# The scan's tile with the place within a chunk outermost

## The reference, cut to what matters

```
Bu = einsum('blh,pht->blpt', x, B_mat)
S = 1 + steps * G
M = [1/S, -alpha/steps, steps/S, 1 - alpha]          # 2x2 per feature
F1 = steps / S * Bu ;  F2 = steps**2 / S * Bu
# state_t = M @ state_{t-1} + (F1_t, F2_t), over the 2048 tokens of a sequence
ys = second component of the state
Cy = einsum('blpt,hpt->blht', ys, C_mat)
out = Cy[..., 0] - Cy[..., 1] + x * D
```

## Time and profile before

| | us |
|---|---|
| median of 3 runs (2365.41 to 2367.84) | 2366.09 |
| the profiled execution, its own time | 2358.44 |
| its span, first to last instruction | 2356.0 |
| PE busy / DVE busy / ACT busy / POOL busy | 2176.4 / 2028.9 / 1542.3 / 671.4 |
| mean granted TensorE clock | 0.956 |

### The profile page before, as it was taken

One profiled execution on the slowest core, in us unless ns is written; L12 is line 12 of the kernel. 1 busy time (PEld: TensorE's weight loads), 2 busy tenths in 40 slices (PEclk: granted clock), 3 DMA queues, 4 the chain that ended last, 5 costly groups with the idle time before them and its releaser, 6 DMA issues. The chain is left out here.

```text
span 2356.0 us, 47793 instructions
## 1 busy us (share of the span) xinstructions
PE 2176.4 (92%) x15828; PEld 1282.4 (54%) x15829; DVE 2028.9 (86%) x5148; ACT 1542.3 (65%) x2993; POOL 671.4 (28%) x997
## 2 busy tenths in 40 slices
PE   4599968999999999999999999999998894999997
PEld 2355544444444444444444544544543783888886
DVE  7799858999999999999999999999991664777775
ACT  3144414678888888888888888888888452444443
POOL 5523002232322322322322322322211254333333
PEclk8799977999999999999999999999999886999999
DMA  5179875654554654432432432433222895444443
GB/s 169 58 217 266 276 179 77 119 118 90 103 107 88 108 107 86 92 84 63 92 85 63 92 78 70 92 76 72 69 89 64 292 307 215 78 81 81 82 81 70
DMA packets 176412, 273.23 MB, mean 116 GB/s; under 512 B 53608, under 2 KB 126072, under 8 KB 170372
## 3 DMA queue, kind: packets, MB, share of 16 engines
q0 software_dynamic: 45840, 137.55, 28.6%
q1 hardware_dynamic: 125332, 122.86, 17.3%
q10 hardware_dynamic: 5044, 10.32, 1.5%
HBM read 128.64 MB, written 140.98 MB: 114 GB/s over the span
## 5 line engine op out<-in xcount | busy, mean ns | idle before, releaser
L1524 ACT ACTIVATE a_p<-banks 128x512 f32<-128x512 f32 x2176 | 1131.2, 608 | 256.8 <-PE banks L1417 206.8
L1577 DVE TENSOR_REDUCE a_mx<-banks 128x1 f32<-128x512 f32 x1536 | 943.4, 680 | 20.1 <-PE banks L1406 20.0
L1485 PE MATMUL banks<-a_p,a_v 128*32 128x512 f32 (+3 forms) x5120 | 589.0, 544 | 1.6 <-ACT a_o L1542 1.1
L1406 PE MATMUL banks<-a_k,a_q 52*128 52x512 f32 (+5 forms) x1600 | 446.8, 413 | 1.9 <-DVE a_rowtop L1574 0.3
L1417 PE MATMUL banks<-a_q,a_k 50*128 50x512 f32 (+7 forms) x1600 | 415.8, 396 | 1.1
L1574 DVE CUSTOM_DVE_ANT_0 a_masked<-banks,a_later 128x512 bf16<-128x512 f32 (+3 forms) x768 | 330.8, 484 | 19.2 <-PE banks L1406 17.3
L1417 PEld LDWEIGHTS banks<-a_q,a_k 54*128 54x128 f32 (+1 forms) x1600 | 227.3, 185 | 198.7 <-DVE a_mx L1577 95.6
L1406 PEld LDWEIGHTS banks<-a_k,a_q 52*128 52x128 f32 (+1 forms) x1600 | 224.1, 185 | 118.0 <-DVE a_mx L1577 55.4
L1406 PE MATMUL banks<-a_k,q 48*128 48x512 f32 (+6 forms) x896 | 256.7, 420 | 6.2 <-DMA a_k<-aug_rows 4.6
L1417 PE MATMUL banks<-q,a_k 50*128 50x512 f32 (+7 forms) x896 | 231.5, 402 | 1.1 <-DVE a_orow L1597 0.3
L1485 PEld LDWEIGHTS banks<-a_p,a_v 128*32 128x32 f32 x5120 | 109.3, 108 | 175.0 <-issue 125.3
(11 more groups left out here) (276 smaller groups left out, 2997.2 us busy)
## 6 DMA issues: line engine op xcount, KB each, us to landing
expert_rows<-a_zeros POOLq DMA_DIRECT2D x132, 258.0 KB, 5.3
a_k<-ka_parts POOLq DMA_DIRECT2D x42, 256.0 KB, 6.3
e_x<-expert_rows SPq DMA_DIRECT2D x71, 129.0 KB, 2.3
expert_rows<-e_y SPq DMA_DIRECT2D x71, 128.0 KB
qa_parts<-m_part SPq DMA_DIRECT2D x16, 512.0 KB
ka_parts<-m_part SPq DMA_DIRECT2D x16, 512.0 KB
va_tiles<-m_va SPq DMA_DIRECT2D x8, 1024.0 KB, 6.8
qb_parts<-m_part SPq DMA_DIRECT2D x16, 512.0 KB, 3.8
```

Source lines behind the costliest of these rows:

```text
L1406: ins = pe.matmul(ps[bank][:, col:col + w], q_op[r % 3][part, p, qt * P:(qt + 1) * P], keys_of(r, k0)[part, kp, k0:k0 + w], start=True, st ...
L1485: ins = pe.matmul(ps_o[VW * h:VW * h + VW, c0:c0 + w], v_op[o][:, kt, hk * VW:hk * VW + VW], prob[:, (at + slot) % NPB, col:col + w], star ...
L1524: nc.scalar.activation(prob[:, (t * NSC + n) % NPB, :], ps[bank][:, :], ACT.Exp, scale=SCALE).then_inc(s_ex, 1)
L1577: ins = v.tensor_reduce(top, ps[bank][:, :], AX.X, ALU.max)
```

## The change

The tile has the same size and place, but its elements are ordered otherwise. Before, token i of chunk c of a partition stood at element 16 c + i. Now it stands at element 256 i + c. A place of all chunks is therefore 256 elements in a row, and the 16 tokens of one chunk are 256 elements (1 KB) apart. Each user of the tile has a view that goes over it in the old order of tokens:

```diff
             def scale(n):
                 act.wait_ge(s_bu, n + 1)
-                nc.scalar.activation(f2[:, n * BT:(n + 1) * BT], bu[n % 2][:, :], ACT.Copy,
+                nc.scalar.activation(by_chunk(f2)[:, n * (BT // CHUNK):(n + 1) * (BT // CHUNK), :],
+                                     bu[n % 2][:, :].rearrange("p (c i) -> p c i", i=CHUNK), ACT.Copy,
                                      scale=C["c2"]).then_inc(s_f, 1)
...
-            f2v = f2[:, :].rearrange("p (c i) -> p c i", i=CHUNK)
+            f2v = by_chunk(f2)
...
+def by_chunk(tile):
+
+    return tile[:, :].rearrange("p (i c) -> p c i", i=CHUNK)
...
-    own = M["f2"][:, :].rearrange("p (b c i) -> p b c i", b=B, i=CHUNK)[:, b, first:first + count, :]
+    own = by_chunk(M["f2"])[:, b * NCH + first:b * NCH + first + count, :]
...
                 for k in range(KD):
-                    pe.matmul(ps[k][:, :], c_mat[:, k * P:(k + 1) * P], y[:, blk * BT:(blk + 1) * BT],
+                    pe.matmul(ps[k][:, :].rearrange("p (c i) -> p c i", i=CHUNK), c_mat[:, k * P:(k + 1) * P],
+                              by_chunk(y)[:, blk * (BT // CHUNK):(blk + 1) * (BT // CHUNK), :],
                               start=True, stop=True).then_inc(s_c, 1)
```

## The result

The changed kernel takes 2374.22 us (median of 7 runs, 2369.08 to 2381.06), the one before 2365.41 (7 runs of its own). The medians are 8.8 us apart. The ratio of the two kernels is given as 1.0042, with a 95% interval from 1.0031 to 1.0053, which is 7.3 to 12.5 us; it is not the quotient of the medians (1.0037). The changed kernel is slower. The forecast was +5.9. Spans are 2368.6 and 2356.0 us.

A forecast was written before the change was run, and what follows sets the result against it. DVE was taken to bound 42 to 72 us, PE the end of `front` and 136.7 to 320 us. Front -7.3, PE's reads +11.8 and POOL's additions +1.4 gave +5.9 us, 2372.0 us; range 2359 to 2380.

The forecast's parts named there:

- The steps on DVE: In `front`: contiguous operands shorten a step from 1.87 to 1.38 us; DVE 7.65 us earlier from L385, range 5.5 to 9.5.
- POOL's part: In `front`: DVE's loss beside POOL's L211, L215 and L217 taken as unchanged, some 2.4 us, from 1 to 5.
- ACT's write: In `front`, before DVE starts: ACT's last write to elements 1 KB apart costs 0.4 us more, once; bounds 0 and 0.43.
- PE's reads: In `middle`: lone words at 1.67 ns cost 0.43 us more a MATMUL, 1.72 a block, +11.8 us in all.
- no cost: Rival for `middle`: PE reads lone words at no cost, hidden by its own pace; -5.9 us, 2360.2; chance 0.23.
- a share of its own cycle: Rival for `middle`: PE pays 0.14 us more a MATMUL, 4.2 us; total -1.7 us, 2364.4; chance 0.1.
- POOL's additions: In `middle`, blocks 0 to 2: L544 and L546 on lone words delay DVE, for which PE waits; +1.4 us, 0 to 5.
- half of 6 x 0.45: In `middle`: six POOL additions in blocks 0 to 2, each 0.45 us longer, half reaching the end: 1.4 us.

The follow-up runs named there:

- TensorE in a row: The changed kernel, with TensorE's first product of a block reading 512 contiguous elements of the normalised input's tile instead of lone words (result wrong): 2359.37 us, ratio 0.9983 to the kernel before.
- the additions in the working tile: The changed kernel, with GpSimd's two additions per block of the carried state going to a contiguous working tile (blocks 1 to 7 lack it): ratio 1.0016 to the kernel before.
- TensorE's lone words alone: The kernel before, with only TensorE's first products reading lone words 1 KB apart, from the normalised input's tile (result wrong): ratio 1.0051, +12.2 us.
- the kernel in fours: The whole computation with four neighbouring tokens side by side, a place of all chunks being every fourth word: 2359.16 us, ratio 1.0005 to the kernel before.
- words 8 bytes apart: The kernel before, with TensorE's first products reading every second word of the normalised input's tile (result wrong): 2362.5 us, a single time.
- 64 bytes: The kernel before, with TensorE's first products reading lone words 64 bytes apart from the normalised input's tile (result wrong): 2366.0 us, a single time.

## Why the prediction was right, and what it mis-sized

- *The steps on DVE:* right. 1.37 us against 1.38 forecast, the copy 0.30 against 0.3. POOL's part was as costly as before (0.3 on L386, 2.0 on L391, and two small ones), as was assumed. `front` got 8.0 us shorter in this pair of executions and 6.8 by the means of the eleven traces, 7.3 forecast.
- *ACT's write:* right, +0.43 us. DVE still starts at 41.81, because this execution had PE's and ACT's last block some 0.5 us earlier, which was not foreseen and belongs to no step.
- *PE's reads:* right in kind and size. 1.67 ns for a lone word gave 0.86 us for a MATMUL, and the sum of 11.8 us stands against 11.7 measured alone. The parts fit less well than the sum: the first stretch grew by 1.3 for a forecast of 0.86, and in block 5, where PE waits for ACT, by 0.1 for 0.6. The thought that the memory sets this pace, not each engine, fits DVE (1.67 ns a lone word), PE (0.86 us for 512, 1.68 ns), and ACT (+0.43 on 512 elements, which is 0.84 ns more on each); POOL's +0.3 is only 0.6 ns more on each. It is a reading of these rows, not shown by itself. The rivals "no cost" and "a share of its own cycle" fell with the rows of 3.61.
- *POOL's additions:* the term that was mis-sized, 1.4 us forecast and 4.3 to 4.4 measured up to the last group, inside the stated 0 to 5. An addition grew by only 0.3 us (a median of 1.27 to 1.59), less than the 0.45 assumed. What was wrong is the step from there to the end, "half of 6 x 0.45": there are 14 such additions, two for each of seven blocks, and all of their growth arrives. Together they took 18.9 us before and 23.1 after, 4.2 more, which is the cost. The forecast counted the blocks 0 to 2 alone. The additions for the blocks 5 and 6 lie beside DVE's normalisation of the blocks 2 and 3, from 136.7 us on, where PE was taken to be the bound. After the change and before:

```profile
153.64 3.28 DVE L882 TENSOR_SCALAR m_xn<-m_x,m_mv,m_rs 128x256 f32<-128x256 f32 x4
```

```profile
153.95 2.68 DVE L875 TENSOR_SCALAR m_xn<-m_x,m_mv,m_rs 128x256 f32<-128x256 f32 x4
```

  The 0.6 us between them is the growth of two additions, and PE's wait for these rows went from 0.81 to 1.41. With TensorE in a row it is 1.45, and with the additions in the working tile 0.57, so the wait follows GpSimd's additions and not TensorE's reads. The blocks 2 and 3 are each 2.3 us further from the next, of which 1.73 is PE's own and 0.6 this. That DVE waits there for whole POOL instructions is a reading of these rows; no run had the additions elsewhere in time.

  Not every long DVE instruction beside POOL is of this kind. In block 1 the addition L853 takes 3.08 us after the change, but the kernel before with TensorE's lone words alone has it too, with POOL's additions as short as ever:

```profile
111.65 3.08 DVE L853 TENSOR_TENSOR m_u<-m_u,m_f 128x512 f32<-128x512 f32 x1
```

```profile
117.23 3.01 DVE L848 TENSOR_TENSOR m_u<-m_u,m_f 128x512 f32<-128x512 f32 x1
```

  Both lie beside POOL's two terms (L547, L541: 2.09 us for the two in either kernel). TensorE's longer group has shifted the two engines against each other.
- *TensorE's clock:* named by no term. Block 1 is 30.3 us from the next, 4.0 more than before, and part of that is the clock. The busy times by window give the granted clock in the third column from the end, for the changed kernel and then the one before:

```profile
120.00:125.00 5.00, 5.00 (x13) 2.47 (x12) 4.83 (x14) 0.70 (x3) 3.51 (x4) 0.80 0.69 206
```

```profile
120.00:125.00 5.00, 3.34 (x14) 2.08 (x15) 4.78 (x8) 0.00 (x0) 3.61 (x4) 1.00 0.38 118
```

  It is 0.80 behind PE's wait of 3.37 us, and the eight L647 took 1.92 us where the kernel before had 1.09. This fall is not of the change: it is there in ten of the thirteen kept traces, among them the kernel in fours and the one before with words 8 bytes apart, whose additions are as before. There block 1 lasts 26.9 and 26.8 us instead of 26.3, so the fall costs 0.5 to 0.6 at the end. The clock fell behind a wait of 2.27 us (64 bytes) and did not behind one of 2.49 (the kernel before). What decides it stays open; it was not tried. GpSimd's 4.4, taken from a kernel with the fall and one without, is some 3.8 without it, an estimate from these rows; its 4.3 is from two kernels that both have it.

The sum was +5.9 for +8.8: the terms for DVE with ACT and for PE right within 0.7 us, and POOL's short by 3. The sign and the mechanism were right for the reason given, and no two large errors cancel.

## What to carry to other kernels

A layout is paid by every engine that reads or writes the tile, so list them all and price each at its own place: here 15 steps of one engine won some 7 us, and 32 instructions of another, the one that bounds the next stage, lost 12. Ask whether a layout serves both: with two f32 words side by side, the reader across the chunks goes 8 bytes at a time and the reader along them gets pairs, and neither pays. And where an engine on the critical path is held up beside a less busy one, count every instruction of the less busy one that grows: here the whole growth of 14 additions, 4.2 us, reached the end.

## What the runs showed of the hardware

- TensorE's f32 multiplication is slowed by its moving operand: 0.43 us for 512 words in a row (1.88 for the four), 0.44 in pairs 1 KB apart (1.91), 0.45 at 8 bytes apart (1.97), and 0.85 to 0.86 at 64 bytes or 1 KB (3.60, 3.61). At 12 and 16 bytes the four take 2.87 and 3.76 us. From 64 bytes to 1 KB the distance did not matter.
- Every second word is as cheap as a row on VectorE too: 0.48 us for 256 elements at 8 bytes apart, 0.67 at 16, 0.65 at 64. Two hits in a row on the same 16 bytes fit the rows of both engines; that the words be adjacent is not needed. On VectorE no step of 12 bytes was tried, so there the limit is only known to lie between 8 and 16. The Trainium skill's note on lines ("SBUF — State Buffer", Door 1: The DMA port swizzle) asks for two hits on a line of 16 bytes, and these rows agree. The same note of the Trainium skill gives 4 fp32 as how far one can stride for free; if that means a step of four words, these rows disagree (1.93 us a step and 3.76 us), and the last free step here is two words. The Trainium skill's statement in "Vector Engine (DVE) Microarchitecture Reference" (Measured stream behaviour on trn2), that only runs of adjacent words go at full rate, is narrower than what VectorE did at 8 bytes.
- 16 bytes apart was the dearest that was tried: 3.76 us on TensorE against 3.61 at 1 KB, and 0.67 on VectorE against 0.65 at 64 bytes.
- VectorE and GpSimd at the same time: VectorE's four L882 took 3.28 us beside additions of 1.58 and 1.55 us, and 2.68 beside additions of 1.27 and 1.27.
